# Cross-attention with a mixture of experts: both heads' masks added by VectorE on the way out of PSUM

## What is computed

```python
x = x + attention(layernorm(x), ctx, ctx, mask)     # 16 heads of 64
    # scores = q k^T / 8, -inf where mask is set; softmax over the 120; times v; @ Wo + bo
x = x + moe(layernorm(x))
    # 8 experts of 1024 (silu), the top 2 of each row, weighted by softmax of x @ Wg
    # + 0.1 * shared expert of 1024 (silu)
```

## Time and profile before

| | |
|---|---|
| median of 3 runs | 635.07 us (635.04 to 635.55) |
| profiled execution | 631.55 us, its span 629.5 us |
| TensorE busy | 604.8 us, 96% |
| VectorE busy | 360.9 us, 57% |
| ScalarE busy | 372.5 us, 59% |
| POOL busy | 324.8 us, 52% |
| chain that ended last | PE 70%, ACT 11%, DVE 7%, POOL 5% |

### The profile page before, as it was taken

How to read it: one execution, slowest core, us unless ns; L and a number is a source line. 1 busy time by engine, 2 the same in 40 slices (tenths; PEclk the granted TensorE clock), 3 DMA queues, 4 the chain that set the end, 5 groups by cost and what they waited for, 6 DMA issues and landing times.

```text
span 629.5 us, 13319 instructions
## 1 busy us (share of the span) xinstructions
PE 604.8 (96%) x4711; PEld 536.4 (85%) x4711; DVE 360.9 (57%) x740; ACT 372.5 (59%) x1036; POOL 324.8 (52%) x347
## 2 busy tenths in 40 slices
PE   6999999999999999899999899999999999999995
PEld 5776797779776886687988789999999999999995
DVE  4676626762686446765897343755555646564632
ACT  4779508671678339747346264948484848484650
POOL 4976517874579439647251700137425653564443
PEclk9999999999999999999999989999999999999999
DMA  8521262356335444300424538996979997989441
GB/s 267 161 68 35 85 168 87 112 169 175 102 118 169 135 166 146 90 1 0 139 73 151 159 116 285 340 308 185 315 209 339 234 347 190 358 221 311 99 102 20
DMA packets 57582, 106.35 MB, mean 169 GB/s; under 512 B 8173, under 2 KB 30734, under 8 KB 55598
## 3 DMA queue, kind: packets, MB, share of 16 engines
q1 hardware_dynamic: 42094, 63.44, 31.8%
q10 hardware_dynamic: 7840, 32.30, 14.0%
q0 software_dynamic: 7584, 9.76, 8.2%
HBM read 80.24 MB, written 26.16 MB: 169 GB/s over the span
## 4 chain that ended last, share of the span: by engine, by line
PE 70%; ACT 11%; DVE 7%; POOL 5%; issue 4%; another core or an unknown queue 2%; POOLq 0%; ACTq 0%; DVEq 0%
ACT pr L1094 7%; PE bank_s L304 4%; PE bank_s L1584 4%; PE bank_t L306 4%; PE bank_t L305 4%; PE bank_t L304 4%; PE bank_s L306 4%; PE bank_s L305 4%; PE bank_q L304 4%; PE bank_m L304 4%; PE bank_q L306 4%; PE bank_q L305 3%; PE bank_m L305 3%; PE bank_m L306 3%; PE bank_k L305 3%
## 5 line engine op out<-in xcount | busy, mean ns | idle before, releaser
L1094 ACT ACTIVATE pr<-bank_s,nmax 128x120 f32<-128x120 f32 x256 | 88.5, 372 | 42.6 <-DVE nmax L674 42.2
L490 POOL TENSOR_TENSOR pr<-pr,rsum 128x480 f32<-128x480 f32 x64 | 62.8, 988 | 60.7 <-DVE rsum L678 60.2
L1006 DVE TENSOR_TENSOR hh_lo<-hbT,hh_hi 128x512 fp32r<-128x512 f32 x78 | 53.9, 692 | 67.1 <-ACT hh_hi L1224 55.7
L597 POOL TENSOR_TENSOR nop<-nop 128x1 f32<-128x1 f32 x39 | 21.6, 553 | 124.2 <-issue 62.7
L1221 ACT ACTIVATE hbT<-bank_s,b_col 128x256 f32<-128x256 f32 (+1 forms) x120 | 42.6, 421 | 67.1 <-issue 26.3
L598 POOL DMA_INDIRECT out_dram<-yw,xs x39 | 66.3, 1700 | 10.4 <-POOL nop L597 8.8
L575 POOL DMA_INDIRECT xs<-rows_d,sorted_i x39 | 43.2, 1107 | 45.2 <-issue 26.5
L1094 ACT ACTIVATION_READ_ACCUMULATOR pr<-bank_s,nmax 128x1 f32 x256 | 55.6, 217 | 0.0
L1224 ACT ACTIVATE hh_hi<-hbT 128x512 fp32r<-128x512 f32 x78 | 49.3, 632 | 2.5
L1073 ACT ACTIVATE qh<-bank_q,bias_t 128x512 f32<-128x512 f32 x32 | 22.6, 706 | 42.5 <-PE bank_q L306 42.5
L1182 ACT ACTIVATE xg<-bank_s,bias_t 128x512 f32<-128x512 f32 x32 | 22.0, 688 | 38.5 <-PE bank_s L306 22.9
(11 more groups left out here) (367 smaller groups left out, 2153.4 us busy)
## 6 DMA issues: line engine op xcount, KB each, us to landing
praw<-in_L_ffn_W SPq DMA_DIRECT2D x32, 256.0 KB, 2.9
w2s<-zg_hi SPq DMA_DIRECT2D x32, 256.0 KB, 3.6
w2s<-zg_lo SPq DMA_DIRECT2D x32, 256.0 KB, 3.9
aT_hi<-w2s SPq DMA_DIRECT2D x32, 256.0 KB
aT_lo<-w2s SPq DMA_DIRECT2D x32, 256.0 KB
w2n_hi<-w2s ACTq DMA_DIRECT2D x6, 1024.0 KB
w2n_lo<-w2s ACTq DMA_DIRECT2D x6, 1024.0 KB
wq_raw<-in_L_ffn_W ACTq DMA_DIRECT2D x5, 1024.0 KB
```

Source lines behind the costliest of these rows:

```text
L490: nc.gpsimd.tensor_tensor(pt, pt, rsum[:, n % 2, h, :].rearrange("p (t a) -> p t a", a=1).broadcast_to([P, GT, SK]), ALU.mult).then_inc(s[ ...
L1006: nc.vector.tensor_tensor(hh_lo[:, n % 2, u, :], hbT[:, i % 4, :], hh_hi[:, n % 2, u, :].bitcast(F32), ALU.subtract).then_inc(s["hh_lo_s"], 1)
L1094: last = nc.scalar.activation(pr[:, n % 2, h, t, :], bank_s[h][:, t * SK:(t + 1) * SK], ACT.Exp, bias=nmax[st], accum_out=ssum[st])
```

## The change

1. **Masks.** TensorE's mask products and the bf16 identity are gone; the score products open and close their own bank. `maxima` has, for each head, an add of bank_s and the mask into pr, a wait for it (new semaphore ms), and the maximum, which now reads pr. `exps` read and write pr in place. `scores(n)` wait for ms of step n-1 where they waited for the exponentials.
2. **Start.** POOL issues the transfers of bo and bs2 behind the first `rsqrt`; VectorE normalizes the rows ahead of the context's low part.
3. **wo pieces** at steps 1, 2, 3, 4 (before 1, 4, 5, 6), and w2's pieces arranged around them.
4. **Gathers.** Eight at first (AHEAD) and not 15; the others tile by tile, eight ahead of the slot at hand.
5. **Last y_out.** Bias times gate is made before the product is there, then one operation does the rest.
6. **expert_down** waits for hh_lo unit by unit within the products, behind its register loads, and not once ahead of them.
7. **Last steps.** q of step 31 at step 29, k of it at step 30, and its k_out behind `pt_out`.

```diff
@@ maxima, VectorE
                     for h in range(2):
                         sc = bank_s[h][:, 0:GT * SK].rearrange("p (t k) -> p t k", t=GT)
+
+                        dve.wait_ge(s["mb"], n // PAIRS + 1)
+                        if n >= 2:
+                            dve.wait_ge(s["tp"], 2 * (n - 2) + h + 1)
+                        nc.vector.tensor_tensor(pr[:, n % 2, h, :, :], sc, maskb[:, :, :], ALU.add).then_inc(s["ms"], 1)
+                        dve.wait_ge(s["ms"], 2 * n + h + 1)
+                        sc = pr[:, n % 2, h, :, :]
                         nc.vector.tensor_reduce(nmax[:, n % 2, h, :], sc, AX.X, ALU.max, negate=True).then_inc(s["mx"], 1)
@@ exps, ScalarE
-                        if n >= 2:
-                            act.wait_ge(s["tp"], 2 * (n - 2) + h + 1)
                         act.wait_ge(s["mx"], 2 * n + h + 1)
...
-                            last = nc.scalar.activation(pr[:, n % 2, h, t, :], bank_s[h][:, t * SK:(t + 1) * SK], ACT.Exp,
+                            last = nc.scalar.activation(pr[:, n % 2, h, t, :], pr[:, n % 2, h, t, :], ACT.Exp,
@@ scores, TensorE
                     for h in range(2):
                         if n:
-                            pe.wait_ge(s["ex"], 2 * (n - 1) + h + 1)
-                        nc.tensor.matmul(bank_s[h][:, 0:GT * SK], identb[:, :], maskb[:, :, :], start=True, stop=False)
+                            pe.wait_ge(s["ms"], 2 * (n - 1) + h + 1)
...
-                                                    kh[r, n % 2, b * SK:(b + 1) * SK], start=False, stop=t == GT - 1)
+                                                    kh[r, n % 2, b * SK:(b + 1) * SK], start=True, stop=True)
@@ POOL, start
-                pool.dma_start(bo_bc[:, :], bo.rearrange("(a n) -> a n", a=1).broadcast_to([P, C])).then_inc(s["bo_in"], 16)
-                pool.dma_start(bs2_bc[:, :], bs2.rearrange("(a n) -> a n", a=1).broadcast_to([P, C])).then_inc(s["bs2_in"], 16)
...
                 rsqrt(0)
+                pool.dma_start(bo_bc[:, :], bo.rearrange("(a n) -> a n", a=1).broadcast_to([P, C])).then_inc(s["bo_in"], 16)
+                pool.dma_start(bs2_bc[:, :], bs2.rearrange("(a n) -> a n", a=1).broadcast_to([P, C])).then_inc(s["bs2_in"], 16)
@@ VectorE, start
+                normalize(x_tile, "ln1", 0, lambda t: xrows[:, t, 0:C])
                 c_turned(0)
-                normalize(x_tile, "ln1", 0, lambda t: xrows[:, t, 0:C])
@@ wo pieces
-                    if n in (1, 4, 5, 6):
+                    if n in (1, 2, 3, 4):
@@ POOL, gathers
-                for q in range(XU):
+                for q in range(AHEAD):
                     gather(q)
...
-                    for q in range(XU, NBLK):
-                        if SLOT_OF[q - XU] == n - 1:
-                            gather(q)
+                    for q in range(TILE0[n] + AHEAD, min(TILE0[n + 1] + AHEAD, NBLK)):
+                        gather(q)
@@ y_out, VectorE
+                    if n == NS - 1:
+
+                        for q in range(TILE0[n], TILE0[n + 1]):
+                            dve.wait_ge(s["yw_s"], q - 1)
+                            nc.vector.tensor_scalar(yb[:, q % 2, :], b2_e, gate(q), None, ALU.mult).then_inc(s["yadd"], 1)
...
+                            nc.vector.scalar_tensor_tensor(out=yw[:, q % YW, :], in0=bank_y[q % 3][:, 0:C], scalar=gate(q), in1=yb[:, q % 2, :],
+                                                           op0=ALU.mult, op1=ALU.add).then_inc(s["yw_s"], 1)
+                        return
@@ expert_down, TensorE
-                    pe.wait_ge(s["hh_lo_s"], UNIT0[n + 1])
...
                             for f in range(NF):
+                                if t == 0 and f % 2 == 0:
+                                    pe.wait_ge(s["hh_lo_s"], UNIT0[n] + f // 2 + 1)
@@ TensorE, last steps
-                    if p < PAIRS - 2 and not (g and p == 0):
+                    if n + 2 == N - 1:
+                        query(n + 2)
+                    elif n + 1 == N - 1:
+                        key(n + 1)
+                    elif p < PAIRS - 2 and not (g and p == 0):
                         qk(n + 2)
```

More of the change, by code:

```diff
@@ L145, in xattn_moe_kernel @@
         NPIECES = NE * NF * C // CW
-        W2_AT = [{0: 0, 1: 0, 4: 0, 5: 0, 6: 0, 12: 2, 20: 2, 26: 2}.get(n, 0 if n > 27 else 2 if n % PAIRS in (0, 7) else 1) for n in range(N)]
+        W2_AT = [{0: 0, 1: 0, 2: 0, 3: 0, 4: 0, 12: 2, 20: 2, 26: 2}.get(n, 0 if n > 27 else 2 if n % PAIRS in (0, 7) else 1) for n in range(N)]
         assert sum(W2_AT) == NPIECES
@@ L231, in xattn_moe_kernel @@
                    ln1 xbo xt ct xt_hi xt_lo ct_hi ct_lo vp v_act v_dve mb qk_q qk_k q_s k_s
-                   sc mx ex rc nrm tp pt pv a_hi a_lo wo_d x2 ln2 dv_st dv_ag dv_rs dv_ms dv_nb
+                   sc ms mx ex rc nrm tp pt pv a_hi a_lo wo_d x2 ln2 dv_st dv_ag dv_rs dv_ms dv_nb
                    ztp z_hi z_lo lg2 l2_s lgt lgc xb2 ws1_in ws2_in ws1_hi ws1_lo ws2_hi ws2_lo hp silu h_hi h_lo_pool h_lo_dve yp half ysum outst outst_last
@@ L327, in xattn_moe_kernel @@
         SORT_AT = 2 * NF + 4
+        AHEAD = 8
         DVE_LO = 2
@@ L509, in _ @@
                 nc.gpsimd.memset(ident[:, :], 0.0).then_inc(s["zeros"], 1)
[L510 to L514, removed]
+                pool.wait_ge(s["zeros"], 4)
+                nc.gpsimd.affine_select(out=ident[:, :], in_=ident[:, :], compare_op=ALU.not_equal, fill=1.0, base=0,
+                                        pattern=[[-1, P]], channel_multiplier=1).then_inc(s["const"], 1)
                 rsqrt(0)
+                pool.dma_start(bo_bc[:, :], bo.rearrange("(a n) -> a n", a=1).broadcast_to([P, C])).then_inc(s["bo_in"], 16)
+                pool.dma_start(bs2_bc[:, :], bs2.rearrange("(a n) -> a n", a=1).broadcast_to([P, C])).then_inc(s["bs2_in"], 16)
                 for i in (2, 3):
@@ L542, in _ @@
                             piece_lo(i)
-                    if n in (1, 4, 5, 6):
-                        c = (1, 4, 5, 6).index(n)
+                    if n in (1, 2, 3, 4):
+                        c = (1, 2, 3, 4).index(n)
                         piece_lo(8, slice(2 * c, 2 * c + 2))
@@ L748, in _ @@
                         residual(g - 1, 1)
-                    if 1 <= p < PAIRS - 1 and n + 1 < N:
+                    if 1 <= p < PAIRS - 1 and n + 1 < N - 1:
                         k_out(n + 1)
@@ L761, in _ @@
                         pt_out(n - 1)
+                    if n + 1 == N - 1:
+                        k_out(n + 1)
                     if g + 1 < G and p == PAIRS - 1:
@@ L1010, in y_out @@
                     e = expert(dve, n)
+                    gate = lambda q: xs[:, q % XU, bass.ds(e + (C + 1), 1)]
+                    b2_e = b2_bc[:, bass.ds(e, 1), :].rearrange("p a c -> p (a c)")
+                    if n == NS - 1:
+                        for q in range(TILE0[n], TILE0[n + 1]):
+                            dve.wait_ge(s["yw_s"], q - 1)
+                            nc.vector.tensor_scalar(yb[:, q % 2, :], b2_e, gate(q), None, ALU.mult).then_inc(s["yadd"], 1)
+                            dve.wait_ge(s["added"], 16 * TILE0[SLOT_OF[q - YW] + 1])
+                            dve.wait_ge(s["yadd"], q + 1)
+                            dve.wait_ge(s[("g2", "g2w")[q - TILE0[n]]], (n + 1, 2 + SEQ[n][1])[q - TILE0[n]])
+                            nc.vector.scalar_tensor_tensor(out=yw[:, q % YW, :], in0=bank_y[q % 3][:, 0:C], scalar=gate(q), in1=yb[:, q % 2, :],
+                                                           op0=ALU.mult, op1=ALU.add).then_inc(s["yw_s"], 1)
+                        return
                     for q in range(TILE0[n], TILE0[n + 1]):
@@ L1016, in y_out @@
                             dve.wait_ge(s["g2w"], 2 + SEQ[n][1])
-                        nc.vector.tensor_tensor(yb[:, q % 2, :], bank_y[q % 3][:, 0:C], b2_bc[:, bass.ds(e, 1), :].rearrange("p a c -> p (a c)"),
-                                                ALU.add).then_inc(s["yadd"], 1)
+                        nc.vector.tensor_tensor(yb[:, q % 2, :], bank_y[q % 3][:, 0:C], b2_e, ALU.add).then_inc(s["yadd"], 1)
                         if q >= YW:
@@ L1332, in scores @@
                 def scores(n):
-                    if n % PAIRS == 0:
-                        pe.wait_ge(s["mb"], n // PAIRS + 1)
                     if n == 0:
@@ L1413, in logits_turn @@
                     last.then_inc(s["lgt"], 1)
-                pe.wait_ge(s["const"], 2)
+                pe.wait_ge(s["const"], 1)
                 warm(10)
@@ L1611, in expert_down @@
                         for f in range(NF):
+                            if f % 4 == 0:
+                                pe.wait_ge(s["hh_lo_s"], UNIT0[n] + f // 4 + 1)
                             h = slice(f % 4 * P, (f % 4 + 1) * P)
```

4 lines of the change are left out of this document (1 added, 3 removed).

## The result

The changed kernel took **664.9 us** (median of 4 runs, 661.1 to 666.7) where the kernel before took 635.1 on the same chip: ratio 1.046, 95% interval 1.0445 to 1.0475. The direction was right; the size was forecast at half (+15.0 against +29.8 us), and the time lies outside the range. The kernel before takes between 626.1 and 635.1 us on the chips used, so every experiment is compared with it on its own chip. Runs more than 1.5% above the fastest of the same kernel are left out of the ratios; that is one run each of e1 (639.6 us) and e4 (641.2).

What follows compares the result with a forecast made beforehand. TensorE was taken to set the pace in attention before the change. The terms -0.5 - 0.2 + 21.7 + 1.0 - 5.1 - 1.95 = +15.0 us, added to 635.07, gave 650.1 us, range 642 to 661.

Steps and rivals of the forecast that it cites:

- the loop: Attention, ScalarE and VectorE: a plain step's loop grows from 5.00 to 6.36 us, longer than TensorE's 5.17.
- each kind of step: Attention steps carrying other work of the group, priced add to add: from 6.67 to 7.67 us, 23.90 with project_out.
- rival "faster": Attention: VectorE's adds run under TensorE's products, so the kernel takes 611.5 us; chance 0.05.
- the steps' sum: Attention, first add of step 1 to that of step 31: 259.4 us against 237.75 before, +21.7.
- the exponentials: Attention, ScalarE: reading SBUF costs each exponential 0 to 0.04 us more; 0.02 taken, 0.16 for a step's eight.
- the start of the exponentials: Attention, ScalarE: the first exponential starts 1.42 us after the first add.
- rival 2: Attention: repeated TensorE waits bring half clock in one step of four, +27 us, 677 us; chance 0.05.
- The gathers that come later: Experts' slots: gathers after the first eight run eight tiles ahead in POOL's idle time, with no cost in the sum.
- the stall: Shared expert: TensorE's 3.41 us wait and half clock behind the burst of 15 gathers vanish with eight, -5.1 us.
- the tail: End of the kernel: -1.3 us at the last down product and -0.64 at the last tile, together -1.95.
- the last y_out: Last tile at the kernel's end: one operation less after its product, -0.64 us.
- The start: Kernel start: earlier normalizing and moved POOL transfers give between 0 and -0.5 us, -0.2 taken.

Runs made afterwards that it cites:

- e1: The changed kernel with its masks back on TensorE, all other edits kept: 634.4 us, 1.010 of the kernel before.
- e4: The kernel before with the gathers of the change and nothing else: 638.4 us, 1.012 of the kernel before.
- e14: The changed kernel with 11 gathers ahead and idle TensorE products before each attend product but the last: 649.1 us, 1.037 of the kernel before.
- e12: The kernel before with the mask of the second head alone on VectorE: 634.7 us, 1.005 of the kernel before.
- e3: The changed kernel with the gathers as before (15 at first, the rest when a buffer comes free): 651.0 us, 1.039 of the kernel before.
- e7: The changed kernel, unchanged, run again on another chip: 664.4 us, 1.054 of the kernel before.
- e13: The changed kernel with 11 gathers ahead and nothing else altered: 651.8 us, 1.041 of the kernel before.
- e9: The changed kernel with its masks back on TensorE and the gathers 11 ahead: 624.2 us, 0.989 of the kernel before.
- e15: The same kernel as e9, repeated on another chip: 623.1 us, 0.996 of the kernel before.
- e2: The kernel before with the masks on VectorE and nothing else: 654.6 us, 1.045 of the kernel before.

## Why the prediction was wrong
**Right:** the loop. That it closes, and its 6.36 us, came out exactly (the last hundredth by luck: the pieces as read add up to 4.99, not 5.00), and each kind of step within 0.1: 24.0 (23.90), 7.36 (7.30), 6.77 (6.67), 7.31 (7.26), 7.72 (7.67), 7.26 (7.16), 7.44 (7.39), 6.84 (6.74), in e14. The rival "faster" had its deciding point where I put it: e12, with one add, has plain steps of 5.68. The miss is in four other places; of the 20.1 us between forecast and profiled execution the gathers' lead has 15.0, the clock 2.5, the steps' sum 1.8, and the small terms the rest.

**Too small by 1.8 us:** the steps' sum, 261.2 at full clock against 259.4. One part is the exponentials. ScalarE in a step of the changed kernel:

```profile
107.22 0.40 ACT L1109 ACTIVATE pr<-pr,nmax 128x120 f32<-128x120 f32 x1 [2.49 <-DVE nmax L678]
107.61 0.38 ACT L1109 ACTIVATE pr<-pr,nmax 128x120 f32<-128x120 f32 x1
...
110.26 1.08 ACT L1096 ACTIVATE xrows<-xall,nbias,rstd 128x256 f32<-128x256 f32 x2
```

Eight take 3.04 us where they took 2.71: 0.04 each, the upper end; I had taken half. The group means do not show it: an exponential takes 382 against 372 ns, and the read of its sum 187 against 217. Against the half that I took this is 0.16 in each of 21 steps, 3.4 us. The sum came out only 1.8 short, so its other pieces were 1.6 too large together; one of them is the start of the exponentials, 1.37 us after the add (105.85 to 107.22) and not 1.42.

**Misjudged:** rival 2. I gave the clock 0.05 and called single waits of 1.2 us harmless, from the earlier trace rows. For waits of that size it held: after the waits of 1.1 us of the plain steps the clock stayed. I did not ask what TensorE waits in the other steps, though my own sum gave it: a step of 7.4 us with little more than 5.2 of products leaves about 2. The last waits ahead of the five falls are 1.92, 1.54, 2.11, 1.54 and 2.48 us. No size tells the two kinds apart: two more waits of 2.1 us, in the same kernel, are followed by full clock. The Trainium skill's page that I cited (TensorE: Matmul & The Clock Gate, "A second HAM failure mode: psum-queue depth-cycling") tells of a clock that goes down and up like this; the trace now agrees, with 0.50 in the window shown. The price was 2.6 us, a tenth of what I gave it: I had let every slow step cost its whole length, and in three of five the slow products fall into time in which TensorE would have waited.

**Wrong, and the largest part:** "The gathers that come later run eight tiles ahead of use, in POOL's idle time." That was costed at nothing without naming the lead. It could be counted from the code: rows are turned two slots ahead of their down product, eight tiles are four wide slots, and a gather is issued behind the scatter-adds of slot n, so one slot is left (9.4 to 12.0 us from rows to rows in e3, from the third slot on), less two scatter-adds, for a transfer through queues that are 0.95 to 1.04 busy from 425 to 445 us. From issue to use it is 8.6 to 9.8 us where TensorE waits in the change, and 5.4 to 9.0 in e4; the burst of e3 lands in 3.3 in the middle. The price is 15 us in the profiled execution, 7.6 in that of e7, 4 to 13 in e4; by medians the change takes 13.2 us more than e13, on another chip, both without a stall. It is zero with a lead of 11 (e9, e13, e15), where rows are used 17.3 us or more after the issue and land within 9.9.

**Smaller:** the stall (-5.1, measured -5.5) was right where I measured, and is not there on every chip. In the tail, expert_down gave 1.6 (last rows turned to the first of the last two tiles: 18.8 us before, 17.2 now) against 1.3 forecast; the last y_out gave nothing (0.64 forecast), since POOL's scatter-add ahead of it was late next. The start gave nothing that can be told from the rest.

## What to carry to other kernels
Before moving work off the busiest engine, close the loop of the others and add up what they do per round: here 5.00 us stood against 5.68, and two operations of 0.68 us had room for one. Where a transfer is issued later than before, count its lead in time from issue to use and compare it with the landing time under the traffic of that stage, not of the stage in which it used to run. And when new waits appear in front of TensorE's products, add them up step by step and not for the typical step alone, and ask which products would run at half clock: here a fall cost 0.9 and 1.3 us where it met the product that the loop waits for, and 0.3 at most elsewhere.

## What was not expected of the hardware
- A gather of 128 rows lands 2.7 to 5.0 us after its issue in the burst (e3) and 2.8 to 10.0 us after it, 6.5 in the middle, beside the weights' transfers (e4).
- Whether a stall of ScalarE and TensorE stands behind 15 gathers in a row depends on the chip: 2.5 to 6.1 us on three, none on another (e2, e3), none on any with eight. The trace names no cause but "remote".
- The same wait of TensorE (2.1 us, in the third step of a group) is followed by half clock in one step of the change and by full clock in two others; in e3 and in the change the five falls are not at the same steps.
- An exponential in place in SBUF takes 10 ns more by its own duration, but 40 ns more from start to start (0.38 against 0.34 us).
